# Moving three of the next pair's S sums inside VectorE's loop body of a two-layer LoRA kernel

## What is computed

```python
def cond(x, language_ids, W, Wr, A, B):          # 8 experts of rank 16
    base = x @ W.T
    logits = x @ Wr.T + 5.0 * one_hot(language_ids)
    topw, topi = top_k(logits, 2)
    gates = scatter(softmax(topw), topi)
    h = einsum('btd,erd->bter', x, A)
    return base + 2.0 * einsum('bter,bte,eor->bto', h, gates, B)

def ffn(x, W, b, A, Bm, Wr):                     # 4 experts of rank 8
    gates = softmax(x @ Wr.T)
    lora = einsum('bser,eor->bseo', einsum('bsi,eri->bser', x, A), Bm)
    return x @ W.T + b + einsum('bse,bseo->bso', 2.0 * gates, lora)

out = x + ffn(cond(x))
```

## Time and profile before

| | us |
|---|---|
| median of 3 runs | 323.12 (322.81 to 323.19) |
| the profiled execution | 323.0 |
| its span | 321.7 |
| TensorE matmul busy in the span | 318.0 (99%) |
| VectorE busy | 262.3 (82%) |
| ScalarE busy | 128.6 (40%) |

### The profile page before, as it was taken

The page is one execution under the profiler, slowest core; times in us unless marked ns, Lnnn a source line. Parts: engine busy times, 40 slices in busy tenths (PEclk is TensorE's granted clock), DMA queues, the critical chain, the costliest instruction groups (busy, mean ns, idle before and its releaser), DMA issues.

```text
span 321.7 us, 5996 instructions
## 1 busy us (share of the span) xinstructions
PE 318.0 (99%) x2246; PEld 311.9 (97%) x2246; DVE 262.3 (82%) x609; ACT 128.6 (40%) x258; POOL 12.0 (4%) x13
## 2 busy tenths in 40 slices
PE   8999999999999999999999999999999999999996
PEld 6999999999999899899999999999999999999996
DVE  3989999898799778988968968877896887888543
ACT  4872846495147236325412503421250350333111
POOL 1001002800000000000000000000000000000000
PEclk9999999999999999999999999999999999999999
DMA  7998000000000312700330150051024006002003
GB/s 277 410 408 286 3 2 0 2 0 2 0 2 0 132 24 46 260 3 0 112 152 1 56 205 0 0 193 68 0 74 187 0 16 245 0 0 112 23 0 131
DMA packets 10705, 27.59 MB, mean 86 GB/s; under 512 B 3166, under 2 KB 4702, under 8 KB 10688
## 3 DMA queue, kind: packets, MB, share of 16 engines
q1 hardware_dynamic: 10256, 26.83, 23.3%
q10 hardware_dynamic: 432, 0.53, 0.5%
HBM read 18.97 MB, written 8.39 MB: 85 GB/s over the span
## 4 chain that ended last, share of the span: by engine, by line
PE 98%; DMA 1%; ACT 0%; DVE 0%; issue 0%; ACTq 0%
PE sums L1310 98%; DMA in<-part 1%; PE sums L1571 0%; ACT rows L549 0%; DVE b_high L806 0%; ACTq L775 0%
## 5 line engine op out<-in xcount | busy, mean ns | idle before, releaser
L1310 PE MATMUL sums<-b_high,a_high 128*128 128x256 f32 (+1 forms) x224 | 45.3, 286 | 0.3 <-DVE b_high L806 0.3
L1310 PE MATMUL sums<-b_low,a_high 128*128 128x256 f32 (+1 forms) x224 | 45.2, 286 | 0.0
L1310 PE MATMUL sums<-b_high,a_low 128*128 128x256 f32 (+1 forms) x224 | 45.0, 286 | 0.0
L1310 PEld LDWEIGHTS sums<-b_high,a_high 128*128 128x128 f32 x224 | 34.6, 189 | 0.8 <-ACT a_high L549 0.7
L1310 PEld LDWEIGHTS sums<-b_low,a_high 128*128 128x128 f32 x224 | 34.7, 189 | 0.0
L1310 PEld LDWEIGHTS sums<-b_high,a_low 128*128 128x128 f32 x224 | 34.5, 188 | 0.1
L1310 PE MATMUL sums<-t_high,s_high 128*128 128x354 f32 x96 | 31.3, 326 | 0.0
L1310 PE MATMUL sums<-t_low,s_high 128*128 128x354 f32 x96 | 31.1, 324 | 0.0
L1310 PE MATMUL sums<-t_high,s_low 128*128 128x354 f32 x96 | 31.1, 324 | 0.0
L1069 DVE TENSOR_TENSOR rows<-sums,rows 128x354 f32<-128x354 f32 x48 | 24.4, 522 | 3.6 <-PE sums L1310 2.9
L1310 PE MATMUL sums<-ct_low,st_high 128*128 128x244 f32 (+1 forms) x80 | 25.6, 320 | 0.0
(11 more groups left out here) (151 smaller groups left out, 846.7 us busy)
## 6 DMA issues: line engine op xcount, KB each, us to landing
stage<-tokens SPq DMA_DIRECT2D x14, 512.0 KB, 4.1
out<-rows SPq DMA_DIRECT2D x14, 512.0 KB, 4.9
in<-part SPq DMA_DIRECT2D x7, 585.0 KB, 8.6
in<-part SPq DMA_DIRECT2D x4, 777.0 KB, 14.9
in<-part SPq DMA_DIRECT2D x4, 265.0 KB, 17.6
rows<-tokens SPq DMA_DIRECT2D x2, 512.0 KB, 13.7
out<-rows SPq DMA_DIRECT2D x3, 192.0 KB, 2.1
c_plain<-gate_proj SPq DMA_DIRECT2D x1, 544.0 KB, 19.2
```

Of the source, the lines that this page charges most:

```text
L1310: return nc.tensor.matmul(out_, lhs, rhs, start=start, stop=stop, skip_group_check=True)
```

## The change

In the loop pairs, three of the four sums for the next pair move. The sum r22n comes directly behind u3n, S1 comes behind r22n, S2 behind n21, and S3 stands directly in front of S4, behind the reduction that gives `neg_max`. Pairs 0, 1 and 7 are as they were (in pair 7 `next_s` issues nothing). No instruction is added or removed.

```diff
                     add_sums(narrow[:, 1, 1, :], narrow_bank(BANK_NB), narrow[:, 1, 0, :]).then_inc(u3n_read, 1)
-                    next_s(S1)
 
                     dve.wait_ge(u3n_read, j - 1)
                     dve.wait_ge(p5n_done, j - 1)
                     add_sums(narrow[:, 1, 1, :], narrow_bank(BANK_NC), narrow[:, 1, 1, :]).then_inc(r22n_read, 1)
-                    next_s(S2)
+                    next_s(S1)
 
                     dve.wait_ge(p4n_done, j - 1)
                     add_sums(narrow[:, 1, 0, :], narrow_bank(BANK_NB), narrow[:, 1, 0, :]).then_inc(n21_out, 1)
-                    next_s(S3)
+                    next_s(S2)
...
                 nc.vector.tensor_reduce(neg_max[:, :], sec[:, :, 0:E2], AX.X, ALU.max,
                                         negate=True).then_inc(neg_max_ready, 1)
+                if turning:
+                    next_s(S3)
                 if second or turning:
                     next_s(S4)
                 dve.wait_ge(y_exp_ready, j + 1)
```

## The result

The changed kernel takes 324.06 us (median of 22 runs, 323.47 to 324.53) against 323.4 us (median of 22 runs) before. The ratio is 1.0019, 95% interval 1.0011 to 1.0027: slower by 0.6 us. The profiled execution took 323.99 us with a span of 322.7.

The account below looks back on a forecast made before the run. The prediction took TensorE's unbroken stream of matmuls (98% of the span) as the bound. 323.0 - 0.145 (gap at p3n) + 0.85 (five pairs at p7n) = 323.7 us against a median of 323.1, range 322.9 to 324.2.

Parts of the forecast that it names:

- The gain at p3n: TensorE's wait for r22n, queued behind S1, disappears: 0.145 us once in the profiled execution, 0 to 0.27 in general.
- the landing come 0.9 us later: Tiles awaited by S1 could land 0.9 us later than 217.27 before n12 and the gating behind it felt it.
- The lateness through the second gating: S3 before S4 takes 0.60 us of VectorE: `y_half` late by 0.39, tails' sum and u2n by about 0.21.
- The 0.19 us of reserve: At `mixed_tails`, the load could start at 208.39 after the late low part of `vt`, and is due at 208.58.
- The price at p7n: u2n, late by 0.21 against 0.04 us of margin, stops TensorE for 0.17 us in each of pairs 3 to 7.
- one hop for all places: TensorE's load starts 0.115 us behind the end of the VectorE operation it really waits for.
- the predicted step of 0.28 to 0.30: Step in front of p7n's weight loads in pairs 3 to 7, with loads starting 0.12 behind u2n's end.
- The costlier sum: Rival: each second-gating sum costs its full 0.69 us, TensorE loses 0.35 in each of five pairs, 324.6 us; chance 0.09.
- "no change": Rival: the lateness never reaches TensorE or is caught up; only the p3n gap goes, 322.9 us; chance 0.13.
- "faster": Rival: average executions lose far more at p3n and nothing is lost at p7n, 322.4 us or less; chance 0.02.
- 0.2% as the smallest difference: Measurement was taken to tell a difference from none above about 0.2%, 0.65 us; "same" got 0.56, "slower" 0.42.

Follow-up runs that it names:

- experiments one: Kernel before the change with only r22n moved in front of S1, S3 kept in its old place: 323.18 us against 323.53, ratio 0.9993.
- eight: Kernel before the change with only r22n moved in front of S1, timed once more: 323.12 us, ratio 0.9992 to the kernel before.
- fourth experiment: Changed kernel with S3's subtraction made twice, the first copy into a buffer part nothing reads: 326.85 us against 323.53 for the kernel before, ratio 1.0116.
- second experiment: Kernel before the change with only S3 moved in front of S4, S1 and S2 left in place: 324.11 us against 323.53, ratio 1.0027.
- seventh experiment: Changed kernel with TensorE waiting ahead of p7n for u2n alone, the wait for the split S3 left out: 323.12 us in a single execution.
- third: Changed kernel with u2n in front of the split of S1: 323.37 us against 323.53 for the kernel before, ratio 0.9995.
- ninth: Kernel before the change with r22n in front of S1 and u2n in front of the split of S1, timed again: 323.32 us, ratio 0.9998.
- six: Changed kernel with TensorE's two waits ahead of p7n swapped, split S3 first, then u2n: 324.71 us in a single execution.

## Why the prediction was right

*The gain at p3n.* Right. The only gap of the profiled execution is gone and S1's landing hurts nobody: n21 and n12 both still wait for TensorE in the changed kernel. In the trace it gave 0.12 to 0.14 us, once. Taken alone (experiments one and eight) it gave 0.07% and 0.08% in time, 0.2 to 0.3 us, near the upper end of the 0 to 0.27 that I kept open; each interval reaches 1. One detail was wrong without effect: the prediction lets the landing come 0.9 us later before n12 feels it. It left out that VectorE also idles ahead of n21. By its own steps S1 could start as late as 218.60, a landing 1.3 us later.

*The lateness through the second gating.* Right in each link: 0.60 for a sum, 0.38 at `y_half` (0.39 expected), 0.19 left at the tails' sum (0.21 expected), nothing lost at `mixed_tails`. The 0.19 us of reserve that the prediction saw at `mixed_tails` rests on a hop of 0.12; with the 0.05 that the fourth experiment shows it is 0.27, so a size was off there that the change did not touch.

*The price at p7n.* 0.17 in five pairs was expected. Pairs 3 to 6 gave 0.15 to 0.18, pair 7 only 0.10, 0.77 instead of 0.85 us in all. In pair 7, which stands outside the loop, the hop is 0.054 and not 0.12. I had taken one hop for all places, so the predicted step of 0.28 to 0.30 was missed there too. The second experiment gives the price in time: 0.27% (1.0016 to 1.0039).

*The rivals.* The costlier sum (0.69 instead of 0.60 each) falls with the 0.60 steps above; "no change" falls with the second experiment, although its idea that a late load is partly caught up is real in a small way (0.055 us at `mixed_tails`, fourth experiment); "faster" falls with the sign of the result. The fourth experiment shows in addition that behind the change there is no hidden reserve: the next 0.60 us of VectorE costs 0.60 of TensorE.

*The number.* 323.7 was expected against 323.12; 324.06 was measured against 323.4. The difference, +0.6, is the same; the level of both is 0.3 us higher over more runs. The prediction was too pessimistic on the measurement: it took 0.2% as the smallest difference that can be told from none, and with 22 runs of each kernel the interval was 0.08% to either side, so 0.19% is well clear of zero. The right total owes a little to luck: the gap at p7n in pair 7 was overrated by 0.07 us and the loss of 0.05 us at `small_y` of pair 2 was not foreseen, and the two nearly cancel.

## What to carry to other kernels

A place where one engine is said to be "99% busy" still has margins, and each should be read in hundredths: end of the producer, plus the hop, against the consumer's due time. Before moving work along a second engine, follow its queue on to the next operation that the busy engine waits for, even into the next iteration, and count what idle time it passes on the way; here 0.60 us became 0.38, then 0.19, then 0.17. Here the work item could be left where it was: moving the critical sum r22n forward alone was enough.

## What the runs showed of the hardware

*The start of an execution varies more than the effect studied.* Laid over the kernel before, the profiled executions stand between -0.28 us (seventh experiment) and +0.77 us (third) after the first 38 weight loads, with the same code. The ninth lost another 0.53 at its 129th load, still in code common to all. The unprofiled executions spread as well: the 22 of the kernel before lie between 322.69 and 325.11. One execution each can't show 0.6 us, and two traces are best compared from the place of the change on.

*Open.* In all six kernels with S3 moved (the change and experiments two, three, four, six and seven) TensorE also loses 0.05 to 0.09 us once, at `small_y` of pair 2, the first pass of the loop. VectorE's first wide sum starts 0.14 us later behind n12 there than in the kernel before, in all six after 0.09 to 0.10 us of idle time, which the other kernels do not have, and no wait is shown for it. In pair 3 that distance is again the same in all kernels. The cause is open, and so is the question of whether u2n in front of the split costs a little time.
